# One depth tile of a Strassen-like product, its matmuls cut into two halves of the array's rows and issued in pairs

## What is computed

```python
def _L0_cond_ref(x, labeler_index, W, lora_A, lora_B_w):      # on x seen as (4, 512, 1024)
    base = jnp.einsum('bsi,oi->bso', x, W)
    low = jnp.einsum('bsi,bir->bsr', x, lora_A[labeler_index])
    return base + jnp.einsum('bsr,or->bso', low, lora_B_w) * (16 / 32)

def _L1_cond_ref(x, adapter_mapping, W, b, lora_As, lora_Bs):  # on x of (8, 256, 1024)
    base_out = jnp.einsum('bti,oi->bto', x, W) + b
    lora_h = jnp.einsum('bti,bir->btr', x, lora_As[adapter_mapping])
    return base_out + jnp.einsum('btr,bro->bto', lora_h, lora_Bs[adapter_mapping]) * 2.0

x = x + _L0_cond_ref(x, itok_B_0_2, L0_cond_W, L0_cond_lora_A, L0_cond_lora_B_w)
x = x + _L1_cond_ref(x, itok_B_0_23, L1_cond_W, L1_cond_b, L1_cond_lora_As, L1_cond_lora_Bs)
```

## Time and profile before

| | us |
|---|---|
| median of three runs (286.69 to 287.08) | 286.77 |
| the profiled execution | 286.75 |
| its span in the profile | 285.0 |
| outside the span | 1.7 |
| PE busy, share of the span | 281.5, 99% |
| PEld busy | 232.9, 82% |
| DVE busy | 222.6, 78% |
| ACT busy | 146.8, 52% |
| POOL busy | 18.2, 6% |
| DMA queue, share of 16 engines | 33% |

### The profile page before, as it was taken

One profiled execution on the slowest core, in us unless ns is written; L12 is line 12 of the kernel. 1 busy time (PEld: TensorE's weight loads), 2 busy tenths in 40 slices (PEclk: granted clock), 3 DMA queues, 4 the chain that ended last, 5 costly groups with the idle time before them and its releaser, 6 DMA issues.

```text
span 285.0 us, 3712 instructions
## 1 busy us (share of the span) xinstructions
PE 281.5 (99%) x1348; PEld 232.9 (82%) x1348; DVE 222.6 (78%) x266; ACT 146.8 (52%) x195; POOL 18.2 (6%) x22
## 2 busy tenths in 40 slices
PE   8999999999999999999999999999999999999996
PEld 6888888888888888878887788878987887788875
DVE  4777999789797779999799989949596876688400
ACT  4675556615155479855594243555585474505021
POOL 0000020000000003120110000003111200000000
PEclk9999999999999999999999999999999999999999
DMA  6689711151344110103340079431222300014213
GB/s 222 216 275 336 272 28 30 28 174 20 131 142 153 18 28 21 28 8 106 121 147 2 22 251 327 184 121 47 59 49 95 103 2 0 0 37 172 89 51 133
DMA packets 23748, 30.26 MB, mean 106 GB/s; under 512 B 7858, under 2 KB 10290, under 8 KB 23730
## 3 DMA queue, kind: packets, MB, share of 16 engines
q1 hardware_dynamic: 23730, 30.03, 33.3%
HBM read 19.01 MB, written 8.39 MB: 96 GB/s over the span
## 4 chain that ended last, share of the span: by engine, by line
PE 99%; DVE 0%; issue 0%
PE ps L1014 97%; PE ps L1009 1%; DVE keep_s L816 0%
## 5 line engine op out<-in xcount | busy, mean ns | idle before, releaser
L1014 PE MATMUL ps<-brh,ar0h 128*128 128x512 f32 (+1 forms) x180 | 68.8, 388 | 0.0
L1014 PE MATMUL ps<-brh,ar0l 128*128 128x512 f32 (+1 forms) x180 | 68.5, 386 | 0.0
L1014 PE MATMUL ps<-brl,ar0h 128*128 128x512 f32 (+1 forms) x180 | 68.4, 386 | 0.0
L242 ACT ACTIVATE brh<-w_B 128x1024 fp32r<-128x1024 f32 (+1 forms) x39 | 38.2, 981 | 48.4 <-PE ps L1014 42.7
L1014 PE MATMUL ps<-brh,ar1h 128*128 128x512 f32 x160 | 62.5, 390 | 0.0
L1014 PE MATMUL ps<-brl,ar1h 128*128 128x512 f32 x160 | 62.5, 390 | 0.0
L1014 PE MATMUL ps<-brh,ar1l 128*128 128x512 f32 x160 | 62.4, 390 | 0.0
L243 DVE TENSOR_TENSOR brl<-w_B,brh 128x1024 fp32r<-128x1024 f32 (+1 forms) x39 | 43.6, 1123 | 10.4 <-ACT brh L242 9.9
L1014 PEld LDWEIGHTS ps<-brh,ar0h 128*128 128x128 f32 x180 | 34.0, 189 | 7.0 <-DVE ar0h L458 0.8
L1014 PEld LDWEIGHTS ps<-brh,ar0l 128*128 128x128 f32 x180 | 33.8, 188 | 7.1 <-DVE ar0l L462 0.3
L1014 PEld LDWEIGHTS ps<-brl,ar0h 128*128 128x128 f32 x180 | 33.8, 188 | 6.2
(11 more groups left out here) (116 smaller groups left out, 347.6 us busy)
## 6 DMA issues: line engine op xcount, KB each, us to landing
w_B<-in_x SPq DMA_DIRECT2D x32, 256.0 KB, 3.6
out_z<-keep_s SPq DMA_DIRECT2D x23, 256.0 KB, 2.2
w_B<-in_w SPq DMA_DIRECT2D x16, 256.0 KB, 4.7
w_A<-in_w SPq DMA_DIRECT2D x16, 256.0 KB, 4.8
out_z<-keep_w SPq DMA_DIRECT2D x8, 256.0 KB, 2.8
stk<-bh SPq DMA_DIRECT2D x48, 32.0 KB, 2.0
raw<-in_a SPq DMA_DIRECT2D x8, 128.0 KB, 2.3
a1raw<-in_a SPq DMA_DIRECT2D x8, 64.0 KB, 2.2
```

The costliest lines, as they stand in the source:

```text
L242: act(waits + spare, lambda e: e.activation(hi, src, ACT.Copy, scale=scale), h, 0.2 + 0.43 * wide)
L1014: ins = eng.matmul(out_ap, lhs, rhs, start=first, stop=False, skip_group_check=True)
```

## The change

Depth tile k = 2 of product 0 no longer goes through `step`. A new function cuts each of its 12 matmuls in two by the contraction's rows, 0 to 63 and 64 to 127. In the first round (`swap` 0) the output tiles i = 0 and 2 take the lower half of the rows and i = 1 and 3 the upper half, all three passes; in the second round (`swap` 1) the halves are exchanged. So neighbouring matmuls always lie in different halves of the array's partitions and in different banks, and both halves add into the same bank only in different rounds. Every matmul of the second round waits for the last ones of the first (tokens ("half", 0, i) on the four matmuls of pass (1, 0), which now increment PE's semaphore); the first of the second round carries these waits, and the later ones find them covered. The order over i is pass by pass now. The plan is told 0.114 us for each of the 24.

```diff
+        def half_steps(n, ks):
+            ends = []
+            for swap in range(2):
+                for k, (a, b), i in itertools.product(ks, PASSES, range(4)):
+                    half = (i + swap) % 2
+                    rows = slice(64 * half, 64 * half + 64)
+                    last = swap == 0 and (k, a, b) == (ks[-1], 1, 0)
+                    pe(ps[bank_of(n, i)][:, :], ar[n % 2][a][rows, i, k, :], b_tile(n, k, b)[rows, :], False,
+                       [tk("A", a, n, k), tk("B", b, n, k)] + ends, ("half", n, i) if last else None)
+                    plan.jobs[-1].took = 0.114
+                ends = [tk("half", n, i) for i in range(4)]
...
-        for k in range(3):
-            for passes in [(one,) for one in PASSES] if k < 2 else [PASSES]:
+        for k in range(2):
+            for passes in [(one,) for one in PASSES]:
                 for i in range(4):
                     step(0, i, k, passes=passes)
+        half_steps(0, (2,))
         for i in range(4):
             step(0, i, 3, ("P", 0, i))
             kept(0, i, tk("P", 0, i))
```

## The result

The changed kernel took 288.84 us (median of six, 287.75 to 289.29), the kernel before 286.87 in the same session (six, 286.69 to 287.08): a ratio of 1.0059, with a 95% interval of 1.0034 to 1.0083. It is slower, by 1.97 us in the medians, where I had forecast 0.82. The ratio is an estimate of its own from the same runs and not the ratio of the two medians (1.0069): by it the loss is 1.69 us (0.98 to 2.38). The median lies 0.04 above the end of my range (288.8); the ratio, applied to the 286.77 that I started from, gives 288.5, inside it.

A forecast was written before the change was run, and what follows sets the result against it. PE was taken to bound the kernel, busy for 281.5 of 285.0 us. The terms 0 + 0.40 + 0.31 + 0.11 gave +0.82 us, forecasting 287.6 us, with a range of 287.2 to 288.8.

The forecast's parts named there:

- The frame: Whole kernel: PE bounds it, and what PE loses at 10.7 us reaches the end in full.
- A pair for a matmul: Depth tile 2: a pair of halves costs what one full matmul costs, 0.227 us; 0 us for 12 pairs.
- the 0.013 us: Each matmul's fixed time beside its columns; at best a pair hides it, -0.16 us for 12.
- In and out: Into and out of the split array: emptied before its division changes, one visit, +0.40 us (0.35 to 0.45).
- The wait between the rounds: Round two's first load waits for round one's last matmul: 0.54 us start to start instead of 0.227, +0.31 us.
- The stagger: Second pair's upper load stands behind the waiting lower matmul, so each round ends later: 0 to 0.22 us, taken 0.11.
- The other engines: ACT, DVE, POOL, SP: no transfer or job added; job order could turn, costed at nothing.
- Loads open within a half: Rival, within each half: loads not hidden under its running matmul, ten more cost 1.1 us; 288.6 us, chance 0.11.
- No overlap at all: Rival, depth tile 2: 24 matmuls of 64 rows run in succession, 2.72 us more; 290.2 us, chance 0.06.
- Not slower: Rival, whole kernel: within 0.2%, fixed time hidden and no stagger, or a cheap wait; +0.55 us, 287.3 us, chance 0.13.
- a cheap wait: Between the rounds: release when the columns are through, 0.31 - 0.18 = 0.13 us; +0.53 in all without stagger.
- The granted clock: Split stretch: emptier array could let the clock fall from 2.4 to 1.2 GHz, 3 us more; in last group, 0.04.

The follow-up runs named there:

- no_wait: Changed kernel, other engines in the old order, second round taking the same halves with no wait between rounds (result incomplete); 288.33 us, 1.35 above the kernel before.
- one_wait: Changed kernel, other engines in the old order, with one wait between the rounds in place of four; 288.05 us against 286.95 for the kernel before.
- fetch_shift: Kernel before, no split, with 13 narrow matmuls of 64 columns added between depth tiles 1 and 2; 289.15 us against 287.21, ratio 1.0067.
- split_shift: one_wait with 13 narrow matmuls of 64 columns added ahead of the split; 289.46 us against 287.21 for the kernel before, ratio 1.0084.
- two_depths: one_wait with depth tiles 1 and 2 both in halves, 48 matmuls in one visit; 287.56 us, one run.

## Why the prediction was right in kind and short in size

**The frame held.** PE bounds the kernel and what it loses early comes through in full: 0.91 us gave 0.76, with an interval of 0.5 to 1.1.

**A pair for a matmul, 0 us: right.** 0.23 us a pair, in every kernel with a split. Not one of the 0.013 us was hidden; a drift of 0.003 a pair came instead.

**In and out, 0.40 us: right.** Here 0.20 going in (0.32 to the first half, and its load open) and 0.20 going out, as `low_d` had shown for 32 rows; no_wait's whole excess is 0.45.

**The wait between the rounds, 0.31 us: mis-sized.** It measured 0.51: from 11.60 to 12.26 us 0.66 in place of 0.227, and the open load. I had put the row of four wait instructions into the upper bound (0.1 us); three of them cost 0.17, as one_wait shows, and 0.03 more goes to the increments.

**The stagger, 0.11 us: near in size by luck, wrong in kind.** Second loads did not stay behind the waiting matmul: the upper half starts 0.01 us behind the lower one in round one and 0.04 in round two. With the drift this makes 0.07. Sum of the stretch: 0.40 + 0.51 + 0.07 = 0.98, against my 0.82 and the measured 0.99.

**The other engines, 0 us: this step failed.** The cover that I named, late operands' margins, held, and the turned orders cost nothing. But I had followed the change through jobs, waits and transfers only. Its 27 instructions are themselves a thing that is moved: they bring the fetches of PE's program 2 to 4 us forward against all else. One then falls amid the small ctile transfers, one on an output's issue, and `low_f`, whose last operand is ready at 146.4 us in the kernel before and whose first matmul starts at 147.45, waits up to 0.5 us; and in nearly all kernels with some 24 or more instructions added the trace has one more fetch, mostly at or just behind the end of the span. fetch_shift has these marks without a split, split_shift loses the waits with one. That the small `ctile` transfers and the issues of outputs are slow beside such a packet, and nowhere else, the 13 profiles show; that the slow ones are what made `low_f`'s operand late follows from the laid-over traces of two kernels, and no run took a packet away. In place of my 0 us the runs show 0.5 to 0.7 us (five kernels, by the ratio), in the profiles 0.05 to 0.93 behind the stretch, mostly at `low_f` (in two_depths at a `low_d`), and 0 to 0.49 at the end. In the profiles in which no packet falls behind the last matmul the time less the span is 1.71 to 1.74 us; in the six with one behind the end of the span it is 1.71 to 2.20, and in five of them over 1.8.

**The rivals.** Loads open within a half (288.6 us) came close to the measured time by chance, not by its mechanism: four loads stand within 0.30 us at the first pair, so a load does go under the running matmul of its own half. The rule of the Trainium skill ("TensorE: Matmul & The Clock Gate", "The mechanism"), that it does so only where the row group differs, is contradicted for halves too. No overlap at all fell likewise. "Not slower" needed a cheap wait; the wait was dearer than the forecast. The granted clock stayed 1.00.

## What to carry to other kernels

A split array gives nothing where the matmuls already fill its rows: a pair of halves costs one full matmul, and each visit costs about 0.4 us for the ways in and out, with 0.35 to 0.54 more for a wait of PE for itself. If such a wait is needed, put the highest count first, so that one wait instruction covers them all. And when a kernel becomes slower far from an edit, lay its trace over one in which PE stands at the same place, find the first job that is late, and look whether an instruction packet has moved there.

## What was not expected of the hardware

Three further waits in a row, soon fulfilled, cost PE 0.17 us. PE seems to look past a matmul that waits for its half of the array: with neighbours in the same half the stretch is 4.03 us, with alternating ones 4.01. And one packet of 16 KB of the instruction queue slows what goes on beside it, a transfer of 16 KB from 1.84 to 2.43 us in the median, the issue of the output near 130 us from 0.42 us to between 1.20 and 1.69. So 26 instructions more in PE's program, with no new transfer at all, put late landings and a slow issue where other engines work, and in the profiled execution 1.05 us behind the last matmul.
